# Value products of two key tiles in one go, twelve exponentials kept, and the PSUM banks dealt out anew

## The reference, cut to what matters

```python
B, C, H, W = 4, 32, 32, 32          # 1024 queries of an image; HEADS = 4, HC = 8
q = _conv(query, Wq[idx], 'SAME').reshape(n, HEADS, HC, -1)      # 1024 columns
k = _conv(token, Wk[idx], 'VALID').reshape(n, HEADS, HC, -1)     # 30 x 30 = 900 keys
v = _conv(token, Wv[idx], 'VALID').reshape(n, HEADS, HC, -1)
w = jax.nn.softmax(jnp.einsum('nhcq,nhcd->nhqd', q, k), axis=-1)
a = jnp.einsum('nhcd,nhqd->nhcq', v, w).reshape(n, CA, hh, ww)
...
pre = jnp.einsum('anchw,gaoc->gnohw', A, Wproj) + b_gates[:, None, :, None, None]
i, f, g, o = sigmoid(pre[0]), sigmoid(pre[1]), tanh(pre[2]), sigmoid(pre[3])
hout = o * jnp.tanh(i * g)
return jnp.einsum('nchw,oc->nohw', hout, W_out) + b_out[None, :, None, None]
```

## Time and profile before

| | us |
| --- | --- |
| runs | 345.29, 346.2, 349.71 |
| median | 346.2 |
| profiled execution: whole time | 348.92 |
| profiled execution: span from the first to the last instruction | 347.0 |
| PE, DVE, ACT, POOL busy | 312.9, 218.6, 176.1, 40.7 |
| mean granted clock of PE, as a share of 2.4 GHz | 0.944 |

### The profile page before, as it was taken

The page is one execution under the profiler, slowest core; times in us unless marked ns, Lnnn a source line. Parts: engine busy times, 40 slices in busy tenths (PEclk is TensorE's granted clock), DMA queues, the critical chain, the costliest instruction groups (busy, mean ns, idle before and its releaser), DMA issues. The chain is left out here.

```text
span 347.0 us, 6971 instructions
## 1 busy us (share of the span) xinstructions
PE 312.9 (90%) x2780; PEld 120.5 (35%) x2787; DVE 218.6 (63%) x484; ACT 176.1 (51%) x338; POOL 40.7 (12%) x50
## 2 busy tenths in 40 slices
PE   5899887999876999999999999999998998995894
PEld 2578332325221222323323233233332222433731
DVE  3990345583865237786878868787784222589935
ACT  1210110343644678887888878878797793300000
POOL 8400000100000000100101001010000106207000
PEclk9999999999855569999999999999999999998999
DMA  7100000027885397000000000000000000000001
GB/s 237 53 4 4 11 0 1 2 50 209 152 119 127 112 247 328 0 3 2 2 2 0 3 2 2 2 2 2 2 0 3 1 2 0 0 2 4 2 2 60
DMA packets 3460, 15.22 MB, mean 44 GB/s; under 512 B 731, under 2 KB 1547, under 8 KB 2883
## 3 DMA queue, kind: packets, MB, share of 16 engines
q1 hardware_dynamic: 3171, 14.67, 15.7%
q0 software_dynamic: 256, 0.11, 0.2%
HBM read 12.21 MB, written 2.37 MB: 42 GB/s over the span
## 5 line engine op out<-in xcount | busy, mean ns | idle before, releaser
L675 ACT ACTIVATE arena_b<-ps 128x512 f32<-128x512 f32 x232 | 125.3, 604 | 36.5 <-PE ps L1162 35.6
L1138 PE MATMUL ps<-arena_a 72*128 72x450 bf16 x256 | 91.5, 394 | 3.9 <-issue 2.5
L1162 PE MATMUL ps<-arena_a 75*128 75x512 bf16 x224 | 86.6, 397 | 4.6 <-DMA arena_a<-mt_sb 3.9
L882 DVE TENSOR_REDUCE mx<-ps 128x1 f32<-128x450 f32 x120 | 69.2, 617 | 6.7 <-PE ps L1138 5.7
L877 DVE CUSTOM_DVE_ANT_0 sums<-ps,relus 128x450 bf16<-128x450 f32 x68 | 42.0, 626 | 42.7 <-PE ps L1138 33.5
L1180 PE MATMUL ps<-arena_b,vt 128*32 128x512 f32 x448 | 61.4, 621 | 0.7 <-ACT arena_b L675 0.7
L1162 PEld LDWEIGHTS ps<-arena_a 75*128 75x128 bf16 x224 | 21.9, 99 | 77.2 <-ACT arena_b L675 43.9
L683 ACT ACTIVATE relus<-ps 128x450 f32<-128x450 f32 x68 | 37.2, 551 | 10.3 <-PE ps L1138 10.3
L1138 PEld LDWEIGHTS ps<-arena_a 72*128 72x128 bf16 x256 | 25.5, 104 | 39.4 <-issue 12.5
L1029 PE MATMUL ps<-arena_a,cst 32*32 32x512 f32 x864 | 28.6, 596 | 1.1 <-ACT arena_a L626 1.1
L999 PE MATMUL ps<-zeros 128*128 128x512 bf16 x82 | 21.3, 398 | 6.7 <-DMA xa<-x 3.8
(11 more groups left out here) (140 smaller groups left out, 237.8 us busy)
## 6 DMA issues: line engine op xcount, KB each, us to landing
arena_b<-wmodes SPq DMA_DIRECT2D x1, 4096.0 KB, 20.2
arena_a<-k_scratch SPq DMA_DIRECT2D x3, 516.8 KB
arena_a<-q_scratch SPq DMA_DIRECT2D x3, 384.0 KB
cst<-consts SPq DMA_DIRECT2D x1, 1045.0 KB, 9.0
k_scratch<-arena_b SPq DMA_DIRECT2D x3, 344.5 KB, 3.7
cst<-consts SPq DMA_DIRECT2D x1, 864.5 KB, 6.9
arena_a<-k_scratch SPq DMA_DIRECT2D x6, 129.2 KB
arena_a<-k_scratch SPq DMA_DIRECT2D x3, 258.4 KB
```

The lines of the kernel that those rows point to most:

```text
L675: nc.scalar.activation(probs[:, n % PRING, :], ps[:, SCORE_RING[n % len(SCORE_RING)], :], ACT.Exp).then_inc(expd, 1)
L882: nc.vector.tensor_reduce(mx[:, a, e:e + 1], bank, AX.X, ALU.max).then_inc(max_read, 1)
L1138: mm(ps[:, block_bank(i), 0:KHALF], qst[0:PAIR_ROWS, e, g, qt * P:(qt + 1) * P], kst[0:PAIR_ROWS, g, at:at + KHALF], start=True, stop=True ...
L1162: last = mm(ps[:, bank, :], kst[0:S_ROWS, g, t * P:(t + 1) * P], qst[0:S_ROWS, e, g, :], start=True, stop=True)
```

## The change

- The plan holds a tile's values back until two tiles have come together (`VALUE_TILES = 2`), or until the rest of a half has come. A half then has four places with values instead of eight: tiles 0 and 1, 2 and 3, 4 and 5, 6 and the rest.
- The ring of exponentials has 12 slots instead of 8 (`PRING`).
- `MAX_RING` gets a fourth bank, 7, and `O_RING` has one bank, 6. The zero products ahead of `gates` 1 write to bank 7 instead of 6.
- To make room in SBUF, `on` takes the home of `xa`, `sums` and the third of `relus` that of `xb`, and `l1s` lies in `arena_b`. Therefore `xb = xc + b_out` is computed later, at the first `out` of the plan.

```diff
-PRING = 8
+PRING = 12
+VALUE_TILES = 2
...
-MAX_RING = (3, 4, 5)
-O_RING = (6, 7)
+MAX_RING = (3, 4, 5, 7)
+O_RING = (6,)
...
-    due, prev, later, step = 0.0, None, [], 0
+    due, prev, later, step, held = 0.0, None, [], 0, []
...
                 if prev and h == min(2, units - 1):
-                    plan.append(("values", *prev))
+                    held.append(prev)
+                    if len(held) == VALUE_TILES or prev[1] == DT:
+                        plan += [("values", *item) for item in held]
+                        held = []
...
-    plan += [("values", *prev)] + [item for _, item in later]
+    plan += [("values", *item) for item in held + [prev]] + [item for _, item in later]
...
-        on = sb("on", [P, 2, HALF])
-        relus = sb("relus", [P, 3, KHALF])
-        sums = sb("sums", [P, 2, KHALF], BF16)
+        relu2 = sb("relu2", [P, 2, KHALF])
...
+        on = xa[:].rearrange("p (a n) -> p a n", a=2)
+        sums = xb[:, 0:KHALF].bitcast(BF16).rearrange("p (a n) -> p a n", a=2)
+        relus = [relu2[:, 0, :], relu2[:, 1, :], xb[:, KHALF:2 * KHALF]]
...
-            nc.vector.tensor_scalar(xb[:], xc[:], c_("bout"), None, ALU.add).then_inc(l1_read, 1)
...
                 elif item[0] == "out":
                     p = item[1]
+                    if p == 0:
+                        link(nc.vector.tensor_scalar(xb[:], xc[:], c_("bout"), None, ALU.add))
...
-                        keep_clock(6, 9)
+                        keep_clock(7, 9)
```

More of the change, by code:

```diff
@@ L257, in build @@
         gb = sb("gb", [P, 3])
-        l1s = sb("l1s", [96, 3, P])
         zeros = sb("zeros", [P, 512], BF16)
@@ L290, in build @@
         planes = arena_b[:, at:at + 3 * PLANE]
-        assert at + 3 * PLANE <= 16384
+        at += 3 * PLANE
+        l1s = arena_b[0:96, at:at + 3 * P].rearrange("p (x o) -> p x o", x=3)
+        assert at + 3 * P <= 16384
         probs = arena_b[:, 0:PRING * HALF].rearrange("p (s n) -> p s n", n=HALF)
@@ L682, in _ @@
                         act.wait_ge(*blocks_read[first_of_pair(diffs[d - 3])])
-                    nc.scalar.activation(relus[:, d % 3, :], ps[:, block_bank(i), 0:KHALF], ACT.Relu
+                    nc.scalar.activation(relus[d % 3], ps[:, block_bank(i), 0:KHALF], ACT.Relu
                                          ).then_inc(max_relu, 1)
@@ L862, in split_max @@
                                         ).then_inc(m_split, 1)
-            dve.wait_ge(l1_read, 5)
+            dve.wait_ge(l1_read, 4)
             for item in plan:
@@ L876, in _ @@
                             dve.wait_ge(*blocks_read[first_of_pair(diffs[d - 2])])
-                        nc.vector.tensor_tensor_reduce(out=sums[:, d % 2, :], in0=bank, in1=relus[:, d % 3, :],
+                        nc.vector.tensor_tensor_reduce(out=sums[:, d % 2, :], in0=bank, in1=relus[d % 3],
                                                        scale=1.0, scalar=-3.0e38, op0=ALU.add, op1=ALU.max,
```

## The result

The changed kernel takes 360.17 us (median of four runs, 359.29 to 361.84), against 347.95 for the one before, measured beside it: a ratio of 1.038 with a 95% interval from 1.032 to 1.043. It is slower by 3.2 to 4.3%. The forecast had the sign and half the size (+6.6 us, measured +12.2), and 360.17 lies outside its range.

A forecast was written before the change was run, and what follows sets the result against it. PE was taken to bound the attention, with ACT hardly keeping up. Terms 4.4 - 0.2 + 0.9 + 0.1 + 1.4 = +6.6 us on the median of 346.2 gave 352.8 us; range 343.5 to 359.

The forecast's parts named there:

- Half 6's last double step: Half 6's last two-tile stretch: value products now stand behind the last maxima's turning, 7.27 us instead of 6.41, +0.9 us.
- Half 7: The last half, without maxima between scores: ACT sets the pace and the stretch gets longer, +1.4 us.
- A longer or shorter stretch at the lower clock: The remaining case, whole kernel: the stretch at the lower clock changes length either way; chance 0.04.
- tile 6 with the rest, gains nothing: Fourth place with values in a half: no gain, as the rest's 128 x 128 product needs no change of form.
- The fourth bank ... I take 0: Fourth bank of maxima: could give 0.2 us a half, 1.5 in all; taken as 0.
- rival (c): Attention: ACT's delay passes through DVE's maxima to PE's blocks, 0.4 us in 19 double steps, +7.6, 360.4 us; chance 0.09.
- ACT's gap: Behind eight value products ACT runs out of scores for 0.9 to 1.4 us; later scores wait, +4.4 us net in halves 0 to 6.
- Rival (a): Attention: ACT keeps up and only the changes of form count, 6.0 us less, 340.2 us; chance 0.15.
- 6.0 us less on PE's list: Value products: three pairs in each of 8 halves save a change of form there and back, 0.25 us each.
- The very first double step ... -0.2: First two-tile stretch of the attention: at the lower clock PE is slow enough for ACT, -0.2 us.
- One bank of sums, twelve slots and `xb`: Other parts of the diff: no cost from any; `xb` taken as 0, up to -0.66 us.

The follow-up runs named there:

- zeros at the turning: The changed kernel with nine zero products on PE while it waits for the split of the last maxima: 358.25 us, ratio 1.029.
- Short maxima: The changed kernel with DVE's plain maxima over 225 of 450 columns and exponentials scaled by 0.01: 359.93 us.
- short exponentials: The changed kernel with every exponential taken over 256 of its 512 columns: 348.09 us; the same edit with VALUE_TILES = 1: 345.08 us.
- single groups: The changed kernel with VALUE_TILES = 1, all other parts of the change kept: 346.78 us, ratio 0.998 to the kernel before.
- both readers quick: The changed kernel with DVE's plain maxima and ACT's exponentials both over half their columns, exponentials scaled by 0.01: 345.81 us.

## Why the prediction was wrong, step by step

**Which part was missed** is read by laying its working out over the halves (us, forecast against the profiled executions):

| stretch | forecast | measured | with the clock held (zeros at the turning) |
| --- | --- | --- | --- |
| up to half 0's rest product | +0.9 | +0.19 | |
| halves 1 to 5 | +2.7 | +4.13 | |
| half 6 | +1.7 | +2.95 | +1.62 |
| half 7 | +1.4 | +3.21 | +1.57 |

(The forecast's rows add up to 6.7 for 6.6 by rounding.)

**The step that failed outright is one that isn't there: PE's clock was taken to stay.** "Half 6's last double step" and "Half 7" priced a longer wait as a wait alone. Their prices were right, +1.7 (with half 6's two other double steps) and +1.4 against +1.62 and +1.57 once the clock is held. But the wait of 2.11 us (1.31 before) was followed by a clock of 1.2 GHz, and a second fall came in half 7: 3.0 us together. "A longer or shorter stretch at the lower clock" had 0.04, and nothing said that the change itself could start one. The medians' further 1.7 us go with lower mean clocks too, in the slower executions; I have no trace of those. What makes the clock fall in one of these places and not in another stays open.

**In halves 1 to 5 two terms were put at nothing.** The forecast there is 4.1 - 2.7 = 1.4 us short, 0.3 a half. The first term is the fourth place: "tile 6 with the rest, gains nothing", and no loss was reckoned. It lasts 24.08 us in the five halves together, before 23.21: +0.87. Short maxima leave it at 24.07, and short exponentials bring it to 23.67. It is dear in halves 1 and 5 (5.07 and 5.06 instead of 4.70 and 4.69), and in half 1 PE waits for a bank whose difference block DVE is still reading (L882):

```profile
163.58 0.36 PE L1145 MATMUL ps<-arena_a 72*128 72x450 bf16 x1 [0.18 <-DVE mx L882]
```

The other 0.6 us are in the double steps, 87.34 instead of 84.08 us: +3.26, of +2.7 reckoned. There DVE has a part, as short maxima take 1.3 us off them.

**"The fourth bank ... I take 0"** belongs to the same miss. It was weighed as a gain over single groups (none there: 346.78 against 347.76) and not as what double groups need. With three banks the kernel is 7 us slower, and even with four DVE holds PE up. A place in half 5, where PE waits for a bank:

```profile
232.72 0.71 DVE L904 STREAM_TRANSPOSE ot<-ps 128x512 f32<-128x512 f32 x1
...
234.26 0.36 PE L1145 MATMUL ps<-arena_a 72*128 72x450 bf16 x1 [0.48 <-DVE mx L887]
```

This is the mechanism of rival (c) in part: the bank's wait is there, but it hits some double steps, and the two dearest of halves 1 to 5 (6.19 and 6.20 us) are those where DVE has other work besides, the turning of the sums here (L904) and the split of the maxima in half 4. I had priced it for all 19 steps at 0.4 with a chance of 0.09, as an extra, and put none of it into the forecast. That (c)'s 360.4 is nearly the measured median is luck: most of what the forecast lacked is the clock.

**"ACT's gap" was right** in kind, and nearly in size. The gap behind value products is 0.94 to 1.7 us in the trace (0.9 to 1.4 forecast), double steps with one difference block last 5.84 (5.82), and ACT's share is 0.88 to 1.21 a half by the runs with short readers, where the forecast had 1.28 (0.53 net, after 0.75 of gain). Rival (a), that ACT keeps up, is refuted by the run with short exponentials.

**"6.0 us less on PE's list" was right, in its size too:** with both readers quick a double step is 0.24 us shorter than two single ones (0.25 reckoned), or 0.72 a half. A half as a whole gains 0.57, since the fourth place takes back 0.15.

**"The very first double step ... -0.2"** and the rest ahead of half 1 came out 0.7 better than reckoned, and that is in part luck: half 0's two other double steps lasted 6.26 us (two difference blocks, 6.25 forecast) and 5.84 (5.82), from 125.91 by 132.17 to 138.01. But I had compared them with steps at the full clock: before, the clock was low until between 127 and 128 us, and the same work took 11.60 instead of 10.96. In the changed kernel's profiled execution it rose between 125 and 126. When it rises differs between executions, and half 1's start with it (142.13 and 143.58 with the same code), so this row can't be judged to better than 1.5 us. One bank of sums, twelve slots and `xb` cost nothing, as forecast.

## What to carry to other kernels

An engine that stands idle for a fifth of the time can still set the pace, if a ring of three buffers lets it hold work for 1.5 us (three exponentials at 0.49) and its supplier goes away for 2.4. Before making a burst on the engine in the middle, lay one burst out against every ring that it feeds: how many buffers, times the reader's pace, against the burst's length. Of two readers the second shows only when the first has been helped, so test them apart and together. And where PE's waits grow, price the clock besides the wait: here 3.0 of 10.5 us.

## What the runs showed that I hadn't expected

- A wait of PE of 2.11 us, in a stretch in which it was busy before and after, was followed by products at half the clock (2.88 us for 1.92). At the same place of the other kernels the clock fell with waits of 2.10, 2.25, 2.40 and 1.64 us, and not with 1.31 (before) and 1.78. Filling the 2.11 us with zero products also took away a second fall, some 17 us after the first.
- Zero products that kept the clock at 2.4 GHz from 90 to 130 us in one kernel's profiled execution didn't in another's with nearly the same instructions there.
